# Twelve row places, one-hots of target stages a ring ahead, and rows of 136 words in a four-layer graph network

## The reference

```python
def segment_sum(src, seg, n): return jax.ops.segment_sum(src, seg, n)   # sum of rows by index

# layer 0: mean of the edge attributes of each node, by SOURCE; three dense layers with batch norm
v_e = segment_sum(edge_attr, src, n) / max(count(src), 1)
out = concat([x, v_e, u]);  3 x (relu(out @ W.T + b), batch norm)
# layer 1: mean of the neighbours' features, by target
agg = segment_sum(x[src], dst, n) / max(degree, 1)
out = relu((agg + x) @ W.T + b)
# layer 2: a message of x[src] and x[dst] by the edge's type, mean by target, update, layer norm, gelu
msg = (concat([x[src], x[dst]]) @ Wmsg[edge_type]) + bmsg;  agg = segment_sum(msg, dst, n) / count
# layer 3: weighted sum of neighbours, by target
msg = (x @ W)[src] * dinv[src] * w * dinv[dst];  out = segment_sum(msg, dst, n) + b; relu, batch norm
# after each layer: x = layernorm(x + out)
```

## Time and profile before

| | before |
|---|---|
| runs, median of 3 | 4043.15 us |
| profiled execution | 4046.68 us |
| its span | 4044.6 us |
| PE busy | 2964.1 us (73%) |
| DVE busy | 2476.0 us (61%) |
| POOL busy | 1921.3 us (48%) |
| ACT busy | 1084.9 us (27%) |
| DMA packets | 736.72 MB, mean 182 GB/s |
| sum stage of layer 0, first load issued to last add | 1137.1 to 1443.8 us |
| layer 1 | 1898.7 to 2208.4 us |
| layer 2 | 2959.0 to 3265.3 us |
| layer 3 | 3707.9 to 3980.6 us |

### The profile page before, as it was taken

One profiled execution on the slowest core, in us unless ns is written; L12 is line 12 of the kernel. 1 busy time (PEld: TensorE's weight loads), 2 busy tenths in 40 slices (PEclk: granted clock), 3 DMA queues, 4 the chain that ended last, 5 costly groups with the idle time before them and its releaser, 6 DMA issues. The chain is left out here.

```text
span 4044.6 us, 87622 instructions
## 1 busy us (share of the span) xinstructions
PE 2964.1 (73%) x22101; PEld 2581.9 (64%) x22102; DVE 2476.0 (61%) x6634; ACT 1084.9 (27%) x3283; POOL 1921.3 (48%) x1876
## 2 busy tenths in 40 slices
PE   7455544444368886876888799999979976887996
PEld 7222322222257756776777499999868866776884
DVE  6666666666667785333777644444447774334887
ACT  0111000000011145554222332222223037788003
POOL 3777777777710034775000067777754005774000
PEclk9999999999999998998999899999989978998998
DMA  5444444444467725786776244444457826776883
GB/s 190 146 141 142 148 143 142 142 148 142 131 193 239 230 66 191 268 274 203 227 234 187 102 155 158 162 158 161 135 168 223 250 70 218 264 274 207 265 265 119
DMA packets 431355, 736.72 MB, mean 182 GB/s; under 512 B 71749, under 2 KB 207566, under 8 KB 430270
## 3 DMA queue, kind: packets, MB, share of 16 engines
q1 hardware_dynamic: 336846, 498.35, 40.4%
q0 software_dynamic: 94448, 237.72, 16.1%
HBM read 486.89 MB, written 294.76 MB: 193 GB/s over the span
## 5 line engine op out<-in xcount | busy, mean ns | idle before, releaser
L1205 PE MATMUL ps<-ring_raw,hot_raw 128*128 128x128 f32 (+2 forms) x8256 | 1033.0, 282 | 191.8 <-DVE hot_raw L1623 130.9
L1205 PEld LDWEIGHTS ps<-ring_raw,hot_raw 128*128 128x128 f32 x8256 | 972.2, 194 | 263.8 <-DVE hot_raw L1623 98.5
L687 POOL DMA_INDIRECT gbuf<-ring_raw,to_blk x731 | 749.1, 1025 | 796.9 <-ACT ring_raw L841 438.8
L639 POOL DMA_INDIRECT slots<-ring_raw,idx_edges x782 | 763.5, 976 | 241.0 <-issue 241.0
L1231 PE MATMUL ps<-big,hot_raw 128*128 x5160 | 585.2, 276 | 21.0 <-ACT ring_raw L841 16.3
L1231 PEld LDWEIGHTS ps<-big,hot_raw 128*128 128x128 f32 x5160 | 579.0, 192 | 27.6 <-issue 27.4
L1119 PE MATMUL ps<-big 128*49 128x343 bf16 (+6 forms) x784 | 263.5, 490 | 404.8 <-DVE big L1519 403.5
L1119 PEld LDWEIGHTS ps<-big 128*49 128x49 bf16 x784 | 113.9, 159 | 547.5 <-DVE big L1519 313.3
L1641 DVE TENSOR_TENSOR big<-big,ps 128x128 f32 (+2 forms) x1032 | 295.1, 286 | 272.9 <-PE ps L1205 230.6
L841 ACT COPY ring_raw<-ps 128x512 f32<-128x512 f32 x473 | 277.4, 588 | 647.3 <-DMA gbuf<-ring_raw,to_blk 417.5
L1623 DVE SCALAR_TENSOR_TENSOR hot_raw<-ring_raw,back,lane_ids 128x512 f32<-128x512 f32 x516 | 385.7, 748 | 90.9 <-DMA ring_raw<-gbuf 44.7
(11 more groups left out here) (260 smaller groups left out, 3409.4 us busy)
## 6 DMA issues: line engine op xcount, KB each, us to landing
ring_raw<-gbuf SPq DMA_DIRECT2D x774, 268.0 KB, 3.2
ring_raw<-slots SPq DMA_DIRECT2D x258, 272.0 KB, 3.3
ring_raw<-in_edge_attr SPq DMA_DIRECT2D x111, 448.0 KB, 3.8
zr<-lane_rows SPq DMA_DIRECT2D x129, 384.0 KB
zt<-lane_rows SPq DMA_DIRECT2D x86, 384.0 KB
pays_raw<-key_rows SPq DMA_DIRECT2D x112, 224.0 KB
big<-src_rows SPq DMA_DIRECT2D x112, 112.0 KB
slots<-ring_raw,idx_edges POOLq DMA_INDIRECT x782
```

What stands on the lines that cost most here:

```text
L639: pool.indirect_dma_start(edges, bass.IndirectOffsetOnAxis(idx_edges[0:n, u, j:j + 1], 0), edge_rows[0:n, u, j, :], None).then_inc(scatter ...
L687: pool.indirect_dma_start(gbuf, bass.IndirectOffsetOnAxis(to_blk[:, t:t + 1], 0), node_rows[:, r, :], None, bounds_check=NBLK - 1, oob_is_ ...
L1205: ins = pe.matmul(bank(r % 3, width), hots[:, r, j * P:(j + 1) * P], rows[:, j, 0:width], start=j == 0, stop=j == BLK - 1)
```

## The change

Three parts. First, in the sum stages of layers 0 and 1 DVE makes the one-hots of two tiles in one instruction from `dst_lane`, as in layers 2 and 3; for that ACT writes `dst_lane` in layer 0 as well (POOL did it after the stage), and DVE waits for `kept`. In all four layers the pair of tiles 2h and 2h+1 of turn i+1 is made right after the add of tile 2h+1 of turn i, and all three pairs of the first turn come before the first add. Second, layers 0 and 1 have twelve places for rows: even turns use the six of before, odd turns six more, five of them in the memory of `B` and one behind the old ring. SP starts with two turns of loads. Loops on SP, ACT and PE run over two turns at a time. Third, an edge's row in `gbuf` is 136 words instead of 134, so a tile is 272 KB instead of 268.

```diff
-ROW_G = D + 6
+ROW_G = D + PAY
...
+        def odd_rows(q, r):
+            n = BLK * (ROW_A if q == 0 else ROW_G)
+            if r == RING - 1:
+                return ring_raw[:, RING * n:(RING + 1) * n]
+            return B[:, 4 * COLS + r * n:4 * COLS + (r + 1) * n]
...
+        def wait_rows(eng, q, h, r, odd):
+            if odd:
+                eng.wait_ge(odd_in[r], h * 16 + (odd_before(q, r) + 16))
+            else:
+                eng.wait_ge(rows_in[r], h * 16 + (16 * fills_before(("g", q), r) + 16))
...
+            def load_turn(q, h, odd, free=True):
+                i = h * 2 + odd
+                at = loaded(at_blk, q, i, SP, MAXB)
+                for r in range(RING):
+                    if free:
+                        sp.wait_ge(products, i * RING + (q * TILES - RING + r + 1))
+                        sp.wait_ge(kept, i * RING + (q * TILES - RING + r + 1))
+                    sp.dma_start(rows_of(q, r, odd), (slots if q == 0 else gbuf)[bass.ds(at[r], P), :]).then_inc(
+                        (odd_in if odd else rows_in)[r], 16)
+
+            def load_wide(q):
+                for odd in range(2):
+                    load_turn(q, 0, odd, q > 0)
+                with sp.Fori(1, ODD) as h:
+                    for odd in range(2):
+                        load_turn(q, h, odd)
+                load_turn(q, ODD, 0)
...
-            steps.link(pool.tensor_tensor(lane_f, key_s[:, :, :, P_SRC],
-                                          back[:, 0, :, None].broadcast_to([P, TILES, BLK]), ALU.add))
...
+            pool.wait_ge(hot_ready, TILES)
+            pool.sem_inc(issued, 1)
...
+            def keep_turn(q, h, odd):
+                i = h * 2 + odd
+                for r in range(RING):
+                    rows = rows_of(q, r, odd).rearrange("p (k w) -> p k w", k=BLK)
+                    wait_rows(act, q, h, r, odd)
+                    if q == 0:
+                        act.copy(pays[:, bass.ds(i * RING + r, 1), :].rearrange("p a (k w) -> p (a k) w", k=BLK),
+                                 rows[:, :, D:ROW_A])
+                    act.activation(dst_lane[:, bass.ds(i * (RING * BLK) + r * BLK, BLK)],
+                                   rows[:, :, D + P_SRC if q == 0 else AW],
+                                   ACT.Identity, bias=back[:, q, bass.ds(i * RING + r, 1)]).then_inc(kept, 1)
...
+                if q < 2:
+                    with pe.Fori(0, ODD) as h:
+                        for odd in range(2):
+                            one_round(h * 2 + odd, h=h, odd=odd)
+                    one_round(RR - 1, h=ODD)
+                    return
...
                 def two_hots(i, h):
                     dve.wait_ge(products, i * RING + (q * TILES + 2 * h + 2))
+                    if q < 2:
+                        dve.wait_ge(kept, i * RING + (RING + q * TILES + 2 * h + 2))
+                        dve.sem_inc(issued, 1)
...
-                        if q < 2 and (more or r < RING - 3):
-                            one_hot(i + (r + 3) // RING, (r + 3) % RING)
-                        if q > 1 and r % 2 and (more or r < 2):
-                            two_hots(i + (r + 3) // RING, (r + 3) % RING // 2)
...
+                        if r % 2 and more:
+                            two_hots(i + 1, r // 2)
+
+                for h in range(RING // 2):
+                    two_hots(0, h)
```

More of the change, by code:

```diff
@@ L76 @@
 FILLS = (("g", 0), ("s", 1), ("g", 1), ("s", 2), ("g", 2), ("s", 3), ("g", 3))
+EVEN, ODD = (RR + 1) // 2, RR // 2
 def fills_before(stage, r):
-    return sum(RR for s in FILLS[:FILLS.index(stage)] if s[0] == "g" or r % LANE_SETS == 0)
+    return sum(EVEN if s in (("g", 0), ("g", 1)) else RR for s in FILLS[:FILLS.index(stage)] if s[0] == "g" or r % LANE_SETS == 0)
 LCOLS = 86
@@ L347, in gnn_kernel, with odd_before @@
         rows_in = [sem(f"rows_in{r}") for r in range(RING)]
+        odd_in = edge_in[0:3] + [sem(f"odd_in{r}") for r in range(3, RING)]
+        def odd_before(q, r):
+            return (16 * ROUNDS if r < 3 else 0) + 16 * ODD * q
+        def wait_rows(eng, q, h, r, odd):
[3 more added lines that the diff above has]
+                eng.wait_ge(rows_in[r], h * 16 + (16 * fills_before(("g", q), r) + 16))
         kept, hot_ready, products, added = sem("kept"), sem("hot_ready"), sem("products"), sem("added")
@@ L654, in _ @@
             pool.wait_ge(at_ready, 1)
[L655 removed]
+            steps.link(pool.tensor_tensor(local0[:, :], key_s[:, :, 0, P_SRC], back[:, 0, :], ALU.add))
             lane_f = dst_lane[:, :].rearrange("p (t k) -> p t k", k=BLK)
[L657 to L658 removed]
             pool.tensor_copy(lanes[:, :], dst_lane[:, :]).then_inc(lanes_ready, 1)
@@ L809, in _ @@
                 place_batch(ROUNDS - 1, u, u < ARING - 1)
-            def keep(q):
-                with act.Fori(0, RR) as i:
-                    for r in range(RING):
-                        act.wait_ge(rows_in[r], i * 16 + (16 * fills_before(("g", q), r) + 16))
-                        if q == 0:
-                            act.copy(pays[:, bass.ds(i * RING + r, 1), :].rearrange("p a (k w) -> p (a k) w", k=BLK),
-                                     slot_rows[:, r, :].rearrange("p (k w) -> p k w", k=BLK)[:, :, D:ROW_A]).then_inc(
-                                kept, 1)
-                        else:
-                            act.activation(dst_lane[:, bass.ds(i * (RING * BLK) + r * BLK, BLK)],
-                                           node_rows[:, r, :].rearrange("p (k w) -> p k w", k=BLK)[:, :, AW],
-                                           ACT.Identity, bias=back[:, 1, bass.ds(i * RING + r, 1)]).then_inc(kept, 1)
+            def keep_turn(q, h, odd):
[9 more added lines that the diff above has]
+                                   ACT.Identity, bias=back[:, q, bass.ds(i * RING + r, 1)]).then_inc(kept, 1)
+            def keep(q):
+                with act.Fori(0, ODD) as h:
+                    for odd in range(2):
+                        keep_turn(q, h, odd)
+                keep_turn(q, ODD, 0)
             def send(layer):
```

41 lines of the change are left out of this document (13 added, 28 removed).

## The result

The changed kernel takes 4021.87 us (median of 6 runs, 4013.52 to 4023.61), the kernel before 4043.12 in the same comparison: a ratio of 0.9952 (95% interval 0.9939 to 0.9965), 21 us less where 46 were forecast. The profiled execution took 4020.74 us, its span is 4018.6, which is 26.0 less than the span of before.

A forecast was written before the change was run, and what follows sets the result against it. DVE's adds were taken to set the pace, with waits for rows in layers 0 and 1. Terms -21.6 - 23.8 - 2.4 + 1 + 1 = -45.8 us gave 3997 us on the median's footing, range 3974 to 4027.

The forecast's parts named there:

- That makes 6.43 us: DVE's turn in layers 0 and 1: layer 3's 6.22 us plus extra queue steps; saves 21.6 and 23.8 us, later start included.
- Twelve places cover the landing: Row loads, layers 0 and 1: six tiles, 6.4 us, cover landing, issue and ACT; the rest costed at nothing.
- ACT and SP hidden: Layers 0 and 1: ACT's 0.52 us a tile stays below DVE's 1.07, SP's loads take 3.0 us a turn; no cost.
- Later start: Three pairs precede the first add: at 1147.1 instead of 1143.5 us in layer 0, 1908.2 instead of 1905.7 in layer 1.
- Layers 2 and 3: One pair moves ahead of the first add: 1.2 us saved each, 2.4 in all; bounds 0 and 8 us a layer.
- Rows of 136 words: Loads and scatters of layers 1 to 3 carry more bytes: 0 to 10 us cost, taken as 1.
- POOL's lists: Lane lists starting before the last products may hold DVE's last operations: between +2.6 and -1.3 us, taken as +1.
- 1.52 against 0.20 us: A DVE operation of 128x49 beside POOL's list operation against POOL idle, read as agreeing with the shared-port rule for two SBUF inputs.
- A: Rival: queue steps hidden, turns of 6.22 us, and deeper one-hots help layers 2 and 3; 3976 us, chance 0.15.
- B: Rival: rows still come late in the long turns of layers 0 and 1, 29 us back; 4026 us, chance 0.13.
- C: Rival: row arrival rate limits layers 0 and 1 whatever the places; +26 us, 4069 us, chance 0.05.
- D: Rival: landing covered, but ACT delays DVE's pairs behind a late tile, so saved and lost cancel; 4043 within 12, chance 0.05.

The follow-up runs named there:

- e1: The kernel before with twelve row places in layers 0 and 1 and nothing else changed; ratio to the kernel before 0.9850.
- a0: The changed kernel run again on a slower chip, as the mark for its set; ratio to the kernel before 0.9952.
- e3: The changed kernel with the six row places of before in layers 0 and 1; ratio to the kernel before 1.0586.
- e6: The kernel before with only the one-hot pairs of layers 2 and 3 made a whole ring ahead; ratio to the kernel before 1.0000.
- e5: The changed kernel with rows of 134 words in layers 1 to 3, as before; ratio to the kernel before 0.9933.
- e4: The changed kernel with GpSimd's lane lists held back until four steps of the second stage's edge means are made; ratio to the kernel before 0.9936.
- e7: The kernel before with twelve places, single one-hots from landed rows a ring ahead, and layers 2 and 3 in the changed order; ratio to the kernel before 0.9825.
- e8: The changed kernel with a single one-hot of 512 words from kept lanes behind every add, instead of pairs; ratio to the kernel before 0.9799.
- e11: e8 without the wait for products ahead of each one-hot, except in a layer's first turn; ratio to the kernel before 0.9781.

## Why the prediction was wrong, step by step

**The step that failed** is the size of VectorE's turn: "That makes 6.43 us". Measured are 6.69 and 6.85. The mechanism was right (VectorE bounds the turn, queue steps ahead of a pair stand on the path); the term was too small. I counted one queue instruction more than in layer 3, 0.09 us, less 0.06 for an add. In truth there are two. These rows of the queue, layer 0 after, are the register sum and the semaphore step (the wait on `kept` together with the increment of `issued`):

```profile
L1678 DVEq ALU_OP  x126: 40/40/40, 1147.3 to 1426.2; - x126
...
L1679 DVEq EVENT_SEMAPHORE  x129: 21/21/24671, 1116.4 to 1426.3; - x129
```

The listing of the change that stands ahead of the prediction has no row for the second, and I read it as the whole; the source has the `sem_inc`. Layer 3 has two steps less there, not one. So 0.19 us a pair in place of 0.07: 3 x 0.19 = 0.57, against the 0.52 by which the turns of layer 0 differ from layer 3's 6.17. In layer 1 there are 0.68: the branch at the turn's end takes 0.26 us to the next step in place of 0.13, and its adds are 0.005 longer. Priced in us: 42 x 0.26 = 10.9 of layer 0's and 42 x 0.39 = 16.4 of layer 1's miss, 27 together, more than the whole miss of 20 on the profiled executions; layers 2 and 3 gave back 8.8 of it. The adds of layers 0 and 1 took 284 and 291 us where the prediction named 276.

**The worse oversight** lies under it. The same part reads a turn of the old kernel as 6.01 us "with no real wait" and the long one as 6.6, a mean of 6.30; a few paragraphs on it gives the new turn 6.43. That the new one-hots make VectorE's own turn longer was in the numbers, and I took the pairs as a gain ("six instructions of 0.75 us a turn become three of 1.23") without asking what the places would bring alone. e1 is the answer: 0.9850.

**Twelve places cover the landing**: right. The waits for rows are gone, e1 and a0 show it from both sides, e3 shows what happens without. **ACT and SP hidden**: right; ACT's busy time in layer 0 doubled, and nothing waited for it behind the start. **Later start**: right, 1146.8 against a forecast of 1147.1, and 2.6 us in layer 1 against 2.5.

**Layers 2 and 3**: forecast 2.4, measured 6.9 + 4.3. In layer 3 the order is worth 0.09 us in each turn, 4 to 5 us in all (e6), within the bounds given, not the value taken. Of layer 2's some 5 us are not the order's, and their cause is open, as e6 shows.

**Rows of 136 words**: right by the stages, 0 to 2 us (e5). **POOL's lists**: forecast +1, bounds -1.3 to +2.6; measured +4.1, out of bounds. I looked at where the lists begin and not at where their two widest operations, 3.9 us each, would fall. The prediction also took 1.52 against 0.20 us as a case of two SBUF inputs; that operation reads one tensor.

The Trainium skill, "SBUF — State Buffer", section "SBUF: two separate sides", has a VectorE operation with two SBUF inputs and a GpSimd operation that reads SBUF lock the port pair against each other: whichever starts first has it to its end, and the other waits. The prediction took only the half in which GpSimd is first. The trace of the changed kernel shows more of the other half: the pairs, of two SBUF inputs, were not held (at most 1.32 us in place of 1.23), and POOL's operations beside them got longer, L703 1.92 us against 1.04 in e4 and L704 1.96 against 1.13 (its spans are rough). The held one-hot of e7, 2.82 us in place of 0.75, shows the first. Held in the changed kernel were the edge means behind, with one tensor in SBUF as input, up to 2.46 us for an operation of 0.28. The Trainium skill has in the same section such a lock for VectorE's two-port modes too; whether the edge means run in one no run here shows.

**The rivals.** A (queue steps hidden, 6.22) is wrong for pairs; for singles the steps are hidden inside a turn (e8, 6.19), though one more shows twice a turn (e11). B and C fall: no wait for rows is left, and e11 draws 269 GB/s where the kernel before drew 234. D falls: the change does what it says. The time lies in the range (3974 to 4027) by B's arm, but B had no part in it.

## What to carry to other kernels

When an in-order engine paces a loop, compare its own turn before and after the edit, start to start and free of waits, before pricing the waits that go; here the clean turn got longer. Busy time misleads: two short operations that alternate with another kind can be issued ahead and overlap, while a merged one that leaves two dependent operations in a row does not. And split a change that has a cure and a rebuild in it: the cure alone was worth three times the whole.

## What the runs showed of the hardware that was not expected

- On VectorE's queue each step (register sum, wait, increment) takes 0.09 to 0.10 us, and how much of it is seen depends on what runs. The second of two adds in a row waits for the first against a register value; its queue step starts 0.04 us after the first add ends (1303.341 and 1303.380 in layer 0), so all behind it is issued late. With a one-hot between, the same steps run beside it (e8).
- The register load of six addresses takes 0.81 and 1.41 us in turn, on every chip and in every kernel here, and turns that wait for nothing else alternate with it by 0.6 us (6.40 and 6.99, 5.84 and 6.43).
- The same code of layer 2 ran at 6.92 or 7.02 us a short turn in different kernels: the step behind the branch at a turn's end comes after 0.13 or 0.23 us (0.26 in layer 1 of the changed kernel). Cause open.
- A one-hot of 0.75 us took 2.82 beside a GpSimd operation of 2.97 (e7), while pairs of 1.23 us in the changed kernel took at most 1.32 and GpSimd's operations beside them up to 0.9 us more.
- Chips differ: scatter and preparation stages are 17 to 27% longer on the slower ones, at lower GB/s, with the changed kernel's turns in layers 0 and 1 the same to 0.01 us. The granted clock in the scatter windows above differs too, 0.94 and 0.84, but is 1.00 in both preparations; what slows the stages is not shown.
